# Heads mixed as finished matrices, sums taken behind searches, counts of shifted scores, and quantising's last product on GpSimd

## What is computed

```python
# stage 2: feed-forward on values rounded to four bits in blocks of 16
def fp4_quant_dequant(x):
    xb = x.reshape(shape[:-1] + (shape[-1] // 16, 16))
    scale = jnp.maximum(jnp.max(jnp.abs(xb), axis=-1, keepdims=True) / 6.0, 1e-12)
    xn = xb / scale
    idx = jnp.searchsorted(_MID, jnp.abs(xn))
    return (_GRID[idx] * jnp.sign(xn) * scale).reshape(shape)
h = silu(fp4_linear(x, w_gate)) * fp4_linear(x, w_up)      # 352 wide
x = x + fp4_linear(h, w_down)
# stage 3: 16 heads of 64, 16 memory keys and values per head
dots = einsum('bhid,bhjd->bhij', q, k) * scale
dots = einsum('bhij,hk->bkij', dots, pre_proj)             # heads mixed
dots = where(causal, neg, dots)
vk = top_k(dots, 64)[0][..., -1:]
attn = softmax(where(dots < vk, neg, dots))
attn = einsum('bhij,hk->bkij', attn, post_proj)            # heads mixed again
out = einsum('bhij,bhjd->bhid', attn, v) @ Wo + bo
# stage 4: 8 routed and 4 shared experts
```

## Time and profile before

| | |
|---|---|
| median of 3 runs | 1097.38 us (1097.16 to 1098.39) |
| profiled execution, its own time | 1097.65 us |
| its span | 1095.9 us |
| busy, share of span | PE 87%, DVE 80%, ACT 68%, POOL 51% |
| mean granted TensorE clock | 0.95 |
| chain that ended last | DVE 47%, PE 27%, issue 12%, ACT 8%, POOL 3% |

### The profile page before, as it was taken

One profiled execution on the slowest core, in us unless ns is written; L12 is line 12 of the kernel. 1 busy time (PEld: TensorE's weight loads), 2 busy tenths in 40 slices (PEclk: granted clock), 3 DMA queues, 4 the chain that ended last, 5 costly groups with the idle time before them and its releaser, 6 DMA issues.

```text
span 1095.9 us, 16200 instructions
## 1 busy us (share of the span) xinstructions
PE 958.0 (87%) x4177; PEld 597.4 (55%) x4177; DVE 881.1 (80%) x2862; ACT 744.5 (68%) x1935; POOL 560.1 (51%) x1186
## 2 busy tenths in 40 slices
PE   8848697859899998998998989988999777999998
PEld 4224355436666666666666666655666565533433
DVE  5967677659999989999998999988999894354444
ACT  5023122289999998999998999977999793412221
POOL 5906562056767766767675676754766571000000
PEclk9968898889999999999999999988999899799999
DMA  7000000000000000000000000000000000000000
GB/s 236 1 0 1 1 1 0 1 1 2 1 2 1 2 2 1 2 1 1 2 2 1 2 2 2 1 1 1 2 1 2 1 2 1 1 0 11 10 10 10
DMA packets 5533, 8.81 MB, mean 8 GB/s; under 512 B 1632, under 2 KB 3232, under 8 KB 5280
## 3 DMA queue, kind: packets, MB, share of 16 engines
q1 hardware_dynamic: 5408, 7.51, 2.1%
HBM read 6.46 MB, written 1.05 MB: 7 GB/s over the span
## 4 chain that ended last, share of the span: by engine, by line
DVE 47%; PE 27%; issue 12%; ACT 8%; POOL 3%; POOLq 1%; DVEq 1%; ACTq 1%; PEldq 0%; PEld 0%; DMA 0%
DVE Ex L957 10%; DVE top L908 7%; DVE mixed L902 6%; DVE Sx L871 4%; DVE unread L889 3%; PE bA L506 2%; PE bBC L506 2%; DVE yk L980 2%; DVE away L896 2%; PE bBC L507 2%; PE bH L525 2%; PE bFGI L525 2%; PE bFGI L507 2%; PE bFGI L394 2%; ACT Ex L642 1%
## 5 line engine op out<-in xcount | busy, mean ns | idle before, releaser
L1177 POOL TENSOR_TENSOR mixed<-Sx,nthr 128x528 f32<-128x528 f32 (+3 forms) x256 | 185.5, 757 | 11.6 <-issue 11.6
L394 PEld LDWEIGHTS bFGI<-spread,Ex 128*128 128x128 f32 x1280 | 155.5, 199 | 64.3 <-POOL spread L1196 60.1
L408 PE MATMUL bH<-turned 128*128 128x512 f32 (+3 forms) x512 | 153.1, 442 | 36.0 <-ACT turned L650 35.6
L394 PE MATMUL bFGI<-spread,Ex 128*128 128x128 f32 x1280 | 165.2, 287 | 20.8 <-POOL spread L1196 20.0
L623 ACT ACTIVATE unread<-Sx,nthr 128x144 bf16<-128x144 f32 (+3 forms) x256 | 143.9, 563 | 24.8 <-POOL nthr L1158 20.9
L408 PEld LDWEIGHTS bH<-turned 128*128 128x128 f32 x512 | 92.0, 189 | 96.5 <-issue 76.1
L631 ACT ACTIVATE unread<-Sx,nthr 128x144 bf16<-128x144 f32 (+3 forms) x256 | 143.4, 566 | 0.0
L957 DVE SCALAR_TENSOR_TENSOR Ex<-mixed,yk,Ex 128x144 f32<-128x144 f32 (+3 forms) x256 | 138.8, 595 | 1.7 <-ACT Ex L642 1.0
L642 ACT ACTIVATE Ex<-Sx,nmax 128x144 f32<-128x144 f32 (+3 forms) x256 | 125.5, 563 | 0.0
L1196 POOL TENSOR_TENSOR spread<-ident,rinv 128x512 f32<-128x512 f32 x64 | 66.6, 1041 | 86.6 <-DVE rinv L960 86.6
L908 DVE MAX8 top<-mixed 128x8 f32<-128x528 f32 (+3 forms) x256 | 110.7, 492 | 0.0
(11 more groups left out here) (295 smaller groups left out, 1887.3 us busy)
## 6 DMA issues: line engine op xcount, KB each, us to landing
xr<-in_xT SPq DMA_DIRECT2D x4, 256.0 KB, 3.6
w_s<-in_w12T SPq DMA_DIRECT2D x1, 1024.0 KB, 6.5
outT<-xc SPq DMA_DIRECT2D x4, 256.0 KB, 2.0
wq_s<-in_WqT SPq DMA_DIRECT2D x1, 512.0 KB, 3.9
wk_s<-in_WkT SPq DMA_DIRECT2D x1, 512.0 KB, 4.3
wv_s<-in_WvT SPq DMA_DIRECT2D x1, 512.0 KB, 4.3
wo_s<-in_Wo SPq DMA_DIRECT2D x1, 512.0 KB, 4.8
w_s<-in_w3T SPq DMA_DIRECT2D x1, 512.0 KB, 6.7
```

The lines of the kernel that those rows point to most:

```text
L394: last = mm(bFGI[:, k * P:k * P + P], Ex[g % 2][:, t, a:a + P], spread[:, t, :], start=True, stop=True)
L408: last = mm(bH[:, jt * P:T], u[:, jt, :], PT[:, at:at + n], start=h + jt == 0, stop=False)
L1177: Gp.tensor_tensor(y[ph][t], Sx[ph][:, t, 0:NT[t]], nthr[ph][1][:, t:t + 1].broadcast_to((P, NT[t])), ALU.add).then_inc(sem("y_ready"), 1)
```

## The change

Five edits.

1. **Mixing.** PE first makes each head's own matrices unmixed, Wk_h^T Wq_h and the like (`head_products`, 64 products of 64 rows, 32 of them 128 wide and 32 of them 16 wide), ACT copies them to `per_head` (128 x 16 heads x 144). SP stores them to DRAM and reads them back turned, so that a partition holds one head (8 groups of 16), PE mixes heads with a block-diagonal 128x128 matrix (`spread_heads`) in ten products of at most 512 columns, ACT copies those in place, and SP takes them through DRAM back into `per_head`. Um is then turned by an eleventh job. POOL's 80 products are gone.
2. **Quantising.** The last product, the block's scale times the rounded values, moves from DVE to POOL for tokens and hidden values (`scale_tokens`, `scale_hidden`), with two buffers `qmax`.
3. **Hidden values of sequence 0** are made inside the fourth token quantising, not behind it.
4. **Counting.** `count` reads y with bias 2^-126 instead of `Sx` with the threshold, tiles from 3 to 0; `flips` also clears bit 30.
5. **Order in the loop.** `take_sum` stands behind `nearest`; `turn_memory` and `memory_copies` stand earlier; the layer norm pieces of stage 3 are placed anew.

```diff
 def mix_jobs():
-    return iter(range(10))
+    for i in range(2):
+        for lo in range(0, PAIRS, 512):
+            yield i, lo, min(PAIRS, lo + 512)
+    yield 2, 0, 2 * D
...
         def _(sp):
...
+            for i in range(2):
+                sp.wait_ge(sem("heads_copied"), 6 * i + 6)
+                sp.dma_start(heads_store[i], per_head[i][:, :, :].rearrange("p h n -> p (h n)")).then_inc(sem(f"heads_stored{i}"), 16)
+            for i in range(2):
+                sp.wait_ge(sem(f"heads_stored{i}"), 16)
+                for k in range(PART):
+                    rows = slice(H * k, H * k + H)
+                    sp.dma_start(turned_heads[i][rows, :].rearrange("p (s n) -> p s n", n=HD),
+                                 heads_store[i][rows, :].rearrange("s (h n) -> h s n", n=HD)).then_inc(sem(f"heads_turned{i}"), 16)
+            for dst, src in loads["w_moe"]:
+                sp.dma_start(dst, src).then_inc(sem("w_moe"), 16)
+            for i in range(2):
+                sp.wait_ge(sem("mix_copied"), 5 * i + 5)
+                sp.dma_start(mixed_store[i], turned_heads[i]).then_inc(sem(f"mix_stored{i}"), 16)
+                sp.wait_ge(sem(f"mix_stored{i}"), 16)
+                for k in range(PART):
...
+                    sp.dma_start(per_head[i][rows, :, :], mixed_store[i][rows, :].rearrange("h (s n) -> s h n", n=HD)).then_inc(sem(f"mix_back{i}"), 16)
...
             def mix(k=1):
...
+                        last = mm(bH[:, 0:hi - lo], spread_heads[i][:, :], turned_heads[i][:, lo:hi], start=True, stop=True)
+                    last.then_inc(sem("mix_done"), 1)
...
-            mix(3)
+            head_products(0)
+            head_products(1)
+            pe.wait_ge(sem("heads_copied"), 12)
...
                 if b == B - 1:
-                    pe.wait_ge(sem("mix_copied"), 10)
+                    pe.wait_ge(sem("h_tok_done"), TT * B)
+                    mix(1)
+                    pe.wait_ge(sem("mix_copied"), 11)
+                    pe.wait_ge(sem("mix_back0"), 16 * PART)
...
             def count(g):
-                act.wait_ge(sem("nthr2_ready"), g + 1)
-                for t in range(TT):
-                    last = nc.scalar.activation(unread[2][:, OFF[t]:OFF[t] + NT[t]], Sx[g % 2][:, t, 0:NT[t]], ACT.Sign, bias=nthr[g % 2][1][:, t:t + 1],
+                for t in (3, 2, 1, 0):
+                    act.wait_ge(sem("y_ready"), TT * g + 4 - t)
+                    last = nc.scalar.activation(unread[2][:, OFF[t]:OFF[t] + NT[t]], y[g % 2][t], ACT.Sign, bias=least[:, :],
                                                 accum_out=over[g % 2][:, t:t + 1])
...
             for b in range(B):
                 dve.wait_ge(sem("x_tok_ready"), b + 1)
+                if b >= 2:
+                    dve.wait_ge(sem("xq_ready"), b - 1)
+                quant_scale(xc[:, b, :], T, b % 2)
+                if b == 3:
+                    hidden(0, (0, 1))
+                quant_step(xc[:, b, :], T, b % 2)
+                if b == 3:
+                    hidden(0, (2, 3))
+                quant_round(xc[:, b, :], T, b % 2).then_inc(sem("x_rounded"), 1)
...
-                V.tensor_scalar(flips[:, :], away[:, :].bitcast(I32), REST, None, ALU.bitwise_or).then_inc(sem("flips_ready"), 1)
+                V.tensor_scalar(flips[:, :], away[:, :].bitcast(I32), REST, TWO, ALU.bitwise_or, ALU.bitwise_xor).then_inc(sem("flips_ready"), 1)
...
+            def scale_back(view, n, k):
+                blocks = view.rearrange("p (g k) -> p g k", k=QB)
+                return Gp.tensor_tensor(blocks, blocks, qmax[k][:, 0:n // QB].unsqueeze(2).broadcast_to((P, n // QB, QB)), ALU.mult)
...
+            for b in range(B):
+                scale_tokens(b)
+            for b in range(B - 1):
+                scale_hidden(b)
+            for i in range(2):
+                pool.wait_ge(sem(f"mix_back{i}"), 16 * PART)
+            Gp.tensor_copy(um_turned[:, :, :], UmT).then_inc(sem("um_gathered"), 1)
```

303 lines of the change are left out of this document (167 added, 136 removed).

## The result

The changed kernel takes **1042.0 us** (median of 4 runs, 1041.8 to 1044.6) against 1097.3 for the kernel before in the same runs: a ratio of 0.9507, 95% interval 0.948 to 0.953. The forecast was 1047 with the range 1037 to 1064. The profiled execution has a span of 1039.7 us and a time of its own of 1041.76.

A forecast was written before the change was run, and what follows sets the result against it. DVE, held up by POOL's products, bounds setup and stage 2; ACT and DVE fill the loop. Gains 18.9 + 18.1 + 5.5 + 2 + 6 = 50.5 us off a 1095.9 span give 1047 us, range 1037 to 1064.

The forecast's parts named there:

- Scans and weights: Setup: without POOL's products beside DVE, scans fall from 13.29 to 8 us and weights from 31.61 to 18.8; together 18.9 gained.
- The rival that DVE doesn't get faster: Scans and weights: the slow instructions had another cause, so 18.9 falls to 3 and the time is 1063; chance 0.04.
- Tokens: Token quantising up to the first hidden reduce: 27.6 us instead of 45.69, gain 18.1, bounds 14 and 21.
- hidden values as late as now behind the last pass: Tokens' stage: case behind the lower bound, a gain of 14 us instead of 18.1.
- Hidden values: Four rounds up to the first fetch, with the last product on POOL: gain 5.5 us, bounds -2 and 8.
- I take one such in the three other rounds: Hidden values: allowance for one down projection slowed behind a PE gap, 3.3 us more, with rounding 2.5.
- Start-up: Start of the head loop: a table load of 1.28 us goes and centring moves; gain 2 us, bounds -2 and 5.
- Loop: Head loop: the new order at three sequence ends leaves 2 to 2.6 of 4.67 us each; gain 6, bounds 2 and 9.
- nothing is waited for: 0: Loop: ACT's count on y never waits for POOL's shift, so this edit gains and costs 0 us.
- The rival of multiplying misses: Loop: the count on shifted scores names ranks wrongly, `redo_missed` runs oftener at 6.4 us each, 1149 with 16; chance 0.02.
- The clock rival: Hidden values: PE's low clock makes all three rounds and the first hidden values late, 8 to 10 us more, 1056; chance 0.2.
- The round trip rival: Stage 2: reading the mixed matrices back through DRAM ends last and Um comes late; put at 1060 us, chance 0.12.

The follow-up runs named there:

- second profile of the changed kernel: The changed kernel measured once more, nothing altered, as the measure for the other runs: 1043.3 us, ratio 0.9532 to the kernel before.
- PE's gaps filled: Changed kernel plus eight 128x512 products on PE that nobody reads, in its gaps of the third and fourth hidden rounds: 1038.1 us, ratio 0.9485.
- both repairs together: Changed kernel with the hidden values' last product back on DVE and eight unread products in PE's gaps: 1037.4 us, ratio 0.9487.

## Why the prediction was right, step by step

- **Scans and weights: right, and shown.** The cause (GpSimd's products beside DVE) holds with both signs: put back, the scan is at 2.06 again; replaced by fills, it stays at 1.22. The step "from above it falls by 0.68 to 1.38" took a price from a pair of sums; the scan fell by 0.84, to 1.22 and not 1.38, so four pairs took 7.1, not 8. Weights, summed from the undisturbed tensors, came out 0.3 off. The rest of the setup was put at 0.8 and gave 2.9, but that part moves by 3 us from run to run, and in the second profile of the changed kernel it gave 1.0. The 12 us that the head products would cost without cover are no row's; here they and their copies lay between 21.9 and 32.7, 10.7 us, beside DVE's work. The rival that DVE doesn't get faster is refuted.
- **Tokens: right in the sum, wrong in a part.** 27.1 against 27.6, and passes of 5.2 to 5.4 against 5.3. Of the 18.6 us three passes gave 13.9, by shorter instructions and one less; GpSimd's products were not put back into this stage, so that they are the cause here too is carried over from the scans and weights. The other 4.7 belong to PE's new order, which no run put back either. The bound of 14 us for "hidden values as late as now behind the last pass" did not apply: moved back there, they cost nothing, since the chain from gate and up ends the stage either way. The step that GpSimd's product falls mostly under the next reduce holds for the tokens.
- **Hidden values: the mechanism right, the pricing of the clock wrong in place.** GpSimd's product took 2.59 (2.5 predicted), two rounds came out to a tenth. The third had the predicted 16.9 only with PE's gaps filled; without, 19.74. The fourth was 14.95 against 16.7, with the slow projection in it that I had left there, and 11.84 without. "I take one such in the three other rounds" was one such, of 2.8 us. The row behind it has 3.3, while the sum took only 2.4 (70.42 less 62.5 is 7.9, entered as 5.5). So the stage came out within 1.4 us because a third round 2.8 too long, a fourth 1.8 too short and this allowance partly cancel, which is luck. What the prediction did not see is that the edit itself loses here: it counted DVE's 1.7 us out and GpSimd's 2.6 in as a small change, while with the clock behind it the step is worth 5.2 us the wrong way.
- **Start-up: right**, 2.0 of 2, and by the stated steps: one table load is left of three (1.28 us each), and from the first fetch the first head's search comes 3.4 later (26.2 instead of 22.9) and the second's 2.0 earlier. It contains 2.2 us of the loss by GpSimd's product too.
- **Loop: the size too small.** Ends of 22.3 and 22.8, in the predicted 22 to 23; ACT waited 1.11 where I took 1.3. With 2 to 2.6 us left of 4.67, the prediction's own terms give 6.2 to 8 for three ends, and it took 6. 7.2 of the 8.3 us are the order, as the run with the old order shows; the rest is within what the loop moves by chance (7.0 in the second profile of the changed kernel).
- **The count: "nothing is waited for: 0" is right against the kernel before, and its reason was not.** "Both kernels count the same signs, so 3 stay": 3 stayed, but only with the new form of the count; with the old one the changed kernel has five, so the two do not count the same. The rival of multiplying misses had the right mechanism (a count that names no rank) and the wrong owner: the danger lay in the old form of the count in the changed kernel, at 28 us for a full search, not 6.4 for a miss.
- **The clock rival** (1056, all three rounds late) fell as a forecast, with one round late of three. As a mechanism it is the largest thing that these runs found left in this kernel: 5.9 us. The Trainium skill says in "TensorE: Matmul & The Clock Gate" (What's actually happening) that the throttled clock is the default and activity lifts it. By that rule idle products should speed the stage up, and they did: clock 0.97 instead of 0.81, 57.62 instead of 63.56.
- **The round trip rival** is refuted: reading the second set three times costs nothing. The 19 us taken for store and read-back were 14 (issue of the store to the landing of the last read, by the median of 6.1).
- **The range** goes down to 1037 "by the bounds of tokens and ends", but these two give 2.9 and 3 us, which is 1041; both contain the 1042.0.
- On GpSimd and DVE, the Trainium skill's "SBUF — State Buffer" (Who interferes with whom) says that a DVE instruction with two SBUF inputs contends with one of GpSimd that reads, not with one that only writes. The two runs with work added on GpSimd agree: a scan of 2.06 beside products, 1.22 beside fills. The same section of the Trainium skill lets some instructions with one input take the shared ports too; the 0.67 and 0.56 beside fills agree. And by the prediction's reading a small instruction behind the reduce should wait for the rest of GpSimd's 2.59 us, about a us; it took 0.94 instead of 0.21.

Four of the kernels beat both: the changed kernel with the hidden values' product on DVE (0.947), that with the tokens' product on DVE too (0.946), the changed one with PE's gaps filled (0.9485), and both repairs together (0.949), against 0.951 and 0.953 for the changed kernel.

## What to carry to other kernels

When one engine's work makes another slow, test it with both signs, the same work put back and a control that occupies the engine but leaves out the suspected part; the length of one instruction gives the answer that the total can't. In a chain that passes through PE, price an added wait with the clock behind it: 1 us more of PE's gap went with 3.8 us more in one round here, closing that gap opened the next, and with the gaps filled the other choice of engine is the better one. An edit priced at nothing can still be what keeps a rare branch from being taken, so run the change without it.

## What the runs showed of the hardware

- DVE's scan of 128x512 takes 1.22 us by itself and 2.06 beside GpSimd's products, 0.84 more, where a sum of two inputs goes from 0.69 to 1.37.
- Beside GpSimd's products back to back, most sums and products of 96x128 (0.29 us alone) take 1.10 to 1.17, about the length of one GpSimd product, while a scan of 512 columns pays 0.84: short instructions pay the most for their size.
- GpSimd's fills leave DVE's two-input instructions alone, but some instructions with one input and a scalar go from 0.29 to 0.56 and 0.67.
- GpSimd multiplies 1408 columns in 2.59 us, where DVE takes 1.63; a small DVE instruction of 88 columns behind the reduce takes 0.94 instead of 0.21 beside it.
- The same six down products took 2.85 us at a granted clock of 1.00, 4.63 at 0.59, 4.93 at 0.56, and 5.49 at 0.50 (fourth round with the hidden values' product on DVE).
- In the changed kernel 1.18 MB were stored in 4 to 5 us and read back in 8 pieces of 16x16x576 bytes, issued over 3.9 us, each landing 6.1 after its issue (median).
